# A conditioned attention and MLP block: ScalarE instead of GpSimd rounds the prepared weights to their high half

## The chip, the cores and the metric
The kernel runs on one core of a Trainium2 chip. The metric is the device time of one execution in microseconds. Five engines work beside each other, each through its own instructions in order: TensorE (PE; PEld is its weight loading), VectorE (DVE), ScalarE (ACT), GpSimd (POOL), and SyncE (SP), which here issues nearly all the DMAs.

## The reference
Input x has 64 batches of 128 tokens with 512 features, and a condition vector of 512 per batch. All is fp32.
```python
h = film(rmsnorm(x, norm1_w), cond, film1_w, film1_b)     # x * (1 + scale) + shift per batch
Q, K, V = h @ q_w + q_b, h @ k_w + k_b, h @ v_w + v_b
attn = softmax(einsum('bnd,bmd->bnm', Q, K) * D ** -0.5)
x = x_in + (einsum('bnm,bmd->bnd', attn, V) @ proj_w + proj_b)
h = film(rmsnorm(x, norm2_w), cond, film2_w, film2_b)
h = gelu(h @ mlp_w1 + mlp_b1, approximate=False) @ mlp_w2 + mlp_b2      # 512 -> 2048 -> 512
return x + h
```

## The kernel before, in words
Products are kept near fp32 accuracy by splitting an operand a into a high half hi (a rounded to the type fp32r) and a low half lo = a - hi, and adding three products, hi*hi, lo*hi and hi*lo. The MLP's two products are computed with seven block products instead of eight (a Strassen-Winograd scheme, P1 to P7), for which sums of the blocks of each weight matrix are needed. These sums and their halves don't depend on the tokens, so they are made once, in the attention stage, written to DRAM scratch (wu for w1, wd for w2), and streamed from there in the MLP.

A short set-up comes first. The attention stage then runs over 16 groups n = 0 to 15 of four batches (512 tokens), on all engines in a fixed written order:
- TensorE: g products (h times the joined query and key weights) 2 and 3, v product 0, scores, v products 1 to 3, transposes of the probabilities (L600), g product 0 of group n + 1, output products 0 and 1 (L609), g product 1 of n + 1, output products 2 and 3. The output products need the transposed probabilities in SBUF (pT_sb). Group 1 also computes the second FiLM product, between v product 2 and v product 3.
- ScalarE: copies g, modulates h of the next group (L761), keep_v(n,0), squares of x of group n + 2 (L753), four exponentials (L866), rounds h of the next group to its high half (L770), keep_v(n,1) to keep_v(n,3) (copies of the value products out of PSUM, L778), copies the transposed probabilities (pT_sb, L886), and the first two g of the next group.
- VectorE: adds output 2 and 3 of group n - 1 to x (L988), key terms (L979, L982), scales x of group n + 1 by the row of reciprocal norms (L957) and modulates it, maxima of the scores, scaling of the probabilities, low half of h (L971), adds output 0 and 1 of group n.
- GpSimd: norm1(n + 2), the reciprocal norms (L461, L464). In groups 1 to 8 it also prepares chunk c = n - 1 of the weights: sum_weights (four block sums, L481 to L486, once the chunk's source w_src has landed) and seven times split_weights, of which each casts the high half into the buffer w_out (L497) and then subtracts it for the low half (L499). norm1(n + 2) stands between the third and the fourth of the seven. PREP_ORDER gives their order: P1, P2 and P4 take a block of w_src itself, P5, P6, P7 and P3 one of the four sums w_sum. w_out has 8 buffers; the cast into one that was used waits for its store.
- SP, at the start of group n: x2 store, second half, of group n - 1 (L286, waits for the addition of output 3 of group n - 1); the seven weight stores of chunk n - 2 (L316; so a chunk is stored one group after it was made); two loads of the source of chunk n - 1 (L301 for w1, L305 for w2), into the single buffer w_src; load of xT of group n + 2; load of x_tok of group n + 3; store of the norms of group n + 2 (L291, waits for GpSimd) and, when that has landed, the load of their row (L295, broadcast); x2 store, first half, of group n.

In group 9 nothing is prepared; SP then loads the first pair of groups for the MLP (hn, L327) once all weight stores have landed, and ScalarE squares it in that group (L787), between keep_v(9,3) and the copy of the transposed probabilities. The MLP follows, 8 pairs of groups; GpSimd there adds residuals and forms norms.

The semaphores that the change touches: w_mixed counts the block sums (4 per chunk), w_hi the high halves, w_split the low ones (7 per chunk each), w_stored the stores of each w_out buffer, film_full the FiLM products.

Of the kernel before, what the change touches and what calls it, by code (L numbers as in the profile page):

```python
# [37 lines left out]
WOUT = 8  # L38
# [40 lines left out]
def cond_block_kernel(nc, x, xT, cols, condT, wqT, wkT, wvT, wp, f1w, f2w, w1, w2, outT, x2T, wu, wd, rs, rs2):  # L79
# [22 lines left out]
    with ExitStack() as ctx:  # L102
# [105 lines left out]
        def weight_blocks(c):  # L208

            if c < CHUNKS // 2:  # L210
                def view(k, r):
                    return w1_src[:, k:k + 2, r, :].rearrange("p t (j c) -> p j t c", c=P)
                return view(0, 0), view(2, 0), view(0, 1), view(2, 1)

            def view(r, d):
                return w2_src[:, :, r, d:d + 2 * P].rearrange("p j (t c) -> p j t c", c=P)
            return view(0, 0), view(1, 0), view(0, 2 * P), view(1, 2 * P)

        def x2_halves(n):

# [225 lines left out]
        @block.gpsimd  # L446
        def _(pool):
            nc.gpsimd.memset(ident[:], 0.0).then_inc(ident_zero, 1)
            pool.wait_ge(ident_zero, 1)
            nc.gpsimd.affine_select(out=ident[:], in_=ident[:], compare_op=ALU.not_equal, fill=1.0,  # L450
                                    base=0, pattern=[[-1, P]], channel_multiplier=1).then_inc(ident_done, 1)
            nc.gpsimd.memset(probs[:, 0, :], 1.0).then_inc(const_done, 1)
            nc.gpsimd.memset(minus_half[:], -0.5).then_inc(const_done, 1)
            nc.gpsimd.memset(eps_sum[:], EPS * D).then_inc(const_done, 1)
            pool.wait_ge(const_done, 3)
            nc.gpsimd.tensor_copy(ones_r[:], probs[:, 0, :]).then_inc(ones_r_done, 1)

            def norm1(m):
                pool.wait_ge(summed, GB * m + GB)
                wait_used(pool, rstd_stored, 16 * m)  # L460
                nc.gpsimd.tensor_tensor(rstd[:], sumsq[:], eps_sum[:].broadcast_to([P, GB]),  # L461
                                        ALU.add).then_inc(eps_added, 1)
                pool.wait_ge(eps_added, m + 1)
                nc.gpsimd.tensor_tensor(rstd[:], rstd[:], minus_half[:].broadcast_to([P, GB]),  # L464
                                        ALU.pow).then_inc(rstd_done, 1)

            def norm2(m):
                pool.wait_ge(stat_read, m + 1)
                wait_used(pool, rstd2_stored, 16 * m)
                nc.gpsimd.tensor_tensor(rstd2[:], sumsq2[:], eps_sum[:].broadcast_to([P, 2 * GB]),  # L470
                                        ALU.add).then_inc(eps2_done, 1)
                pool.wait_ge(eps2_done, m + 1)
                nc.gpsimd.tensor_tensor(rstd2[:], rstd2[:], minus_half[:].broadcast_to([P, 2 * GB]),
                                        ALU.pow).then_inc(rstd2_done, 1)

            def sum_weights(c):

                a11, a12, a21, a22 = weight_blocks(c)
                s1, s2, s3, s4 = (w_sum[q][:] for q in ("P5", "P6", "P7", "P3"))
                pool.wait_ge(w_src_loaded, 32 * c + 32)  # L480
                nc.gpsimd.tensor_tensor(s1, a21, a22, ALU.add).then_inc(w_mixed, 1)  # L481
                nc.gpsimd.tensor_tensor(s3, a11, a21, ALU.subtract).then_inc(w_mixed, 1)
                pool.wait_ge(w_mixed, 4 * c + 1)
                nc.gpsimd.tensor_tensor(s2, s1, a11, ALU.subtract).then_inc(w_mixed, 1)
                pool.wait_ge(w_mixed, 4 * c + 3)
                nc.gpsimd.tensor_tensor(s4, a12, s2, ALU.subtract).then_inc(w_mixed, 1)  # L486

            def split_weights(c, i):
                q, u = PREP_ORDER[i], 7 * c + i
                a11, a12, _, a22 = weight_blocks(c)  # L490
                src = {"P1": a11, "P2": a12, "P4": a22}[q] if q in ("P1", "P2", "P4") else w_sum[q][:]
                both = w_out[u % WOUT]
                if q == "P5":
                    pool.wait_ge(w_mixed, 4 * c + 4)
                if u >= WOUT:
                    pool.wait_ge(w_stored[u % WOUT], 16 * (u // WOUT))
                nc.gpsimd.tensor_copy(both[:, :, :, 0, :], src).then_inc(w_hi, 1)  # L497
                pool.wait_ge(w_hi, u + 1)
                nc.gpsimd.tensor_tensor(both[:, :, :, 1, :], src, both[:, :, :, 0, :].bitcast(F32),  # L499
                                        ALU.subtract).then_inc(w_split, 1)  # L500

            norm1(0)
            norm1(1)
            for n in range(GROUPS):
                if n == 11:
                    norm2(0)
                if 1 <= n <= CHUNKS:
                    if n == 1:
                        pool.wait_ge(film_full, 2)
                    sum_weights(n - 1)  # L510
                    for i in range(7):
                        if i == 3:
                            norm1(n + 2)
                        split_weights(n - 1, i)
                elif n + 2 <= LAST:
                    norm1(n + 2)

            def add_residual(p, into, rows, half, source, ready, count):

                pool.wait_ge(ready, count)  # L520
                for dt in range(2):
                    block_ap = into[:, 2 * rows + dt, TOK * half:TOK * half + TOK]
                    nc.gpsimd.tensor_tensor(block_ap, source[:, dt, :], block_ap, ALU.add).then_inc(pre_added, 1)  # L523

            for p in range(PAIRS):
                if p < PAIRS - 1:
                    norm2(p + 1)
                pool.wait_ge(b2_added, 8 * p + 8)
                add_residual(p, xres, 0, 1, u2, down_u2, 2 * p + 2)
                add_residual(p, xres, 1, 0, u2, down_u2, 2 * p + 2)  # L530
                add_residual(p, xres, 1, 1, vsum, down_v, 2 * p + 2)
# [216 lines left out]
        def _(act):  # L748
# [16 lines left out]
            def h_high(m, k):  # L765
# [3 lines left out]
                    act.wait_ge(h_done_act, 2 * m + k - 1)  # L769
                nc.scalar.copy(h_hi[m % 2][:, k, :], h[m % 2][:, k, :]).then_inc(h_hi_done, 1)  # L770

            def keep_g(n, j):
                act.wait_ge(g_full, GB * n + j + 1)
                nc.scalar.activation(g[:, j, :], gv[j][:], ACT.Identity, bias=wk_bq[:, j:j + 1]).then_inc(g_read, 1)  # L774

            def keep_v(n, b):
                act.wait_ge(v_full, GB * n + b + 1)
                nc.scalar.copy(v[:, b, :], gv[b][:]).then_inc(v_read, 1)  # L778
# [71 lines left out]

            for n in range(GROUPS):
                keep_g(n, 2)
                keep_g(n, 3)
                if n < LAST:
                    wait_used(act, scored, n)
                    if n == 0:
                        act.wait_ge(cols_read, 2)
                    modulate(n + 1, 2)
                    modulate(n + 1, 3)
                wait_used(act, out_full, GB * n)  # L860
                keep_v(n, 0)
                if n + 2 <= LAST:
                    sum_squares(n + 2)
                act.wait_ge(bias_done, n + 1)
                for b in range(GB):
                    nc.scalar.activation(probs[:, b, :], score_b[:, b, :], ACT.Exp, bias=exp_bias[:, b:b + 1],  # L866
                                         scale=SCALE, accum_out=den[:, b:b + 1]).then_inc(exp_done, 1)
                if n < LAST:
                    for k in range(KD):
                        h_high(n + 1, k)  # L870
                for b in range(1, GB):
                    keep_v(n, b)
                if n == 9:
                    squares_of_pair(0, sq_attn)
                if n == 13:
                    modulate_pair(0, 2)
                    modulate_pair(0, 3)
                if n == 14:
                    act.wait_ge(x2_stored[1], x2_halves(13))
                    for q in SPLIT_ORDER[:3]:  # L880
                        operand_high(0, q)
                if n == LAST:
                    for q in SPLIT_ORDER[3:]:
                        operand_high(0, q)
                act.wait_ge(pT_full, n + 1)
                nc.scalar.copy(pT_sb[:], pT[:]).then_inc(pT_read, 1)  # L886
                if n < LAST:
                    keep_g(n + 1, 0)
                    keep_g(n + 1, 1)
# [364 lines left out]
```

## Time and profile before

| | |
|---|---|
| time, median of 3 runs | 1972.0 us (1967.91 to 1976.14) |
| the profiled execution | 1968.15 us, span 1966.4 us |
| mean granted TensorE clock | 0.965 |
| busy: TensorE, VectorE, ScalarE, GpSimd | 94%, 64%, 44%, 15% |
| GpSimd instructions | 250, of them 56 casts (L497) and 56 subtractions (L499) of weights |
| attention stage | from about 70 us to about 610 us |
| weight preparation on GpSimd | 124 to 389 us |

How to read it: the span runs from the first to the last instruction of one execution; the time of the run has what lies around it as well. A row of a list of instructions begins with its start, then its duration, engine, line, operation, output and inputs, how many instructions are merged in it (x4), and in brackets the idle time of the engine just before and what ended it. Such a row's duration is that of the merged run.

### The profile page before, as it was taken

Reading aid. Unit: us, or ns where it says so; the run is one execution under the profiler, and the core shown is the slowest. Engines: PE = TensorE matmul, PEld = TensorE weight load, DVE = VectorE, ACT = ScalarE, POOL = GpSimd, SP = SyncE. Lnnn points to the kernel's source line nnn. Section 1 sums busy time; section 2 is a strip of 40 time slices with the busy share of each in tenths; the row PEclk is TensorE's granted clock in tenths of the full one; section 3 lists DMA queues with packets and bytes.
Section 4 is the critical chain, followed back from the end, with each engine's and each line's share of the span. In section 5 each row is a group of like instructions: output and inputs, shape, how many; then the busy total and the mean of one; then the engine's idle time right before and its main releaser. Section 6 shows DMA issues by size and latency. Waiting matters only on the chain.

```text
span 1966.4 us, 23402 instructions
## 1 busy us (share of the span) xinstructions
PE 1855.5 (94%) x8596; PEld 1534.7 (78%) x8596; DVE 1260.5 (64%) x1575; ACT 860.1 (44%) x1458; POOL 304.4 (15%) x250
## 2 busy tenths in 40 slices
PE   9999999989998999999899999989999998999998
PEld 8887887868787777777777777777877777787887
DVE  3455564645654687489468748946964894687467
ACT  3435343354633363355236335523633553363353
POOL 0044656600000002002000200200010020001002
PEclk7999999999999999999899999999998999999999
DMA  7237575653224667666666766676776667676775
GB/s 268 83 129 268 177 287 211 237 191 124 75 85 142 192 228 248 182 176 222 228 192 225 249 181 178 225 235 189 231 242 177 177 219 239 189 234 215 205 233 182
DMA packets 204992, 391.86 MB, mean 199 GB/s; under 512 B 22096, under 2 KB 26192, under 8 KB 204880
## 3 DMA queue, kind: packets, MB, share of 16 engines
q1 hardware_dynamic: 204592, 390.11, 61.6%
q8 instruction: 70, 1.15, 0.3%
q14 instruction: 42, 0.34, 0.1%
q10 hardware_dynamic: 288, 0.26, 0.0%
HBM read 327.32 MB, written 62.98 MB: 198 GB/s over the span
## 4 chain that ended last, share of the span: by engine, by line
PE 60%; DVE 14%; POOL 9%; DMA 8%; issue 4%; ACT 3%; SPq 2%; DVEq 0%; POOLq 0%; ACTq 0%
PE ps L639 25%; PE ps L659 13%; PE ps L537 8%; PE ps L667 7%; POOL w_out L499 4%; DMA ring<-wd_scratch 4%; DVE stage_lo L1130 3%; DVE hn L1006 3%; DMA w_src<-w_dram 3%; POOL w_out L497 2%; PE ps L609 2%; PE ps L573 1%; PE ps L578 1%; PE ps L574 1%; ACT hn L793 1%
## 5 line engine op out<-in xcount | busy, mean ns | idle before, releaser
L639 PE MATMUL ps<-op_hi_P,ring 128*128 128x512 f32 x1792 | 573.5, 402 | 15.4 <-ACT p_copy L898 12.9
L659 PE MATMUL ps<-stage_hi,ring 128*128 128x512 f32 x1792 | 447.6, 391 | 15.2 <-DMA ring<-wd_scratch 15.2
L639 PEld LDWEIGHTS ps<-op_hi_P,ring 128*128 128x128 f32 x1792 | 345.4, 195 | 97.2 <-ACT p_copy L898 17.8
L659 PEld LDWEIGHTS ps<-stage_hi,ring 128*128 128x128 f32 x1792 | 336.7, 189 | 90.3 <-DMA ring<-wd_scratch 18.6
L639 PE MATMUL ps<-op_lo_P,ring 128*128 128x512 f32 x896 | 357.4, 399 | 0.0
L819 ACT CAST stage_hi<-x 128x1024 fp32r<-128x1024 f32 x224 | 234.6, 1051 | 247.2 <-PE ps L659 229.2
L1130 DVE TENSOR_TENSOR stage_lo<-x,stage_hi 128x1024 fp32r<-128x1024 f32 x224 | 298.9, 1338 | 50.1 <-ACT stage_hi L819 50.0
L803 ACT ACTIVATE x<-x,vecs 128x512 f32<-128x512 f32 x192 | 138.1, 723 | 382.5 <-DVE x L1117 382.5
L667 PE MATMUL ps<-stage_lo,ring 128*128 128x512 f32 x896 | 245.2, 396 | 16.7 <-DVE stage_lo L1130 16.7
L667 PEld LDWEIGHTS ps<-stage_lo,ring 128*128 128x128 f32 x896 | 165.9, 189 | 62.7 <-DVE stage_lo L1130 29.4
L639 PEld LDWEIGHTS ps<-op_lo_P,ring 128*128 128x128 f32 x896 | 173.4, 194 | 37.7
L523 POOL TENSOR_TENSOR xres<-u,xres 128x512 f32<-128x512 f32 x32 | 70.7, 2239 | 824.5 <-DVE u L1141 824.5
L1117 DVE TENSOR_TENSOR x<-ps,u 128x512 f32<-128x512 f32 x128 | 86.4, 690 | 118.4 <-PE ps L639 118.0
L1136 DVE TENSOR_TENSOR x<-x,x 128x1024 f32<-128x1024 f32 x96 | 134.2, 1398 | 0.0
L1117 DVE TENSOR_TENSOR u<-ps,p_copy 128x512 f32<-128x512 f32 x64 | 44.2, 691 | 138.8 <-ACT p_copy L898 71.3
L774 ACT ACTIVATE g<-ps,wk_bq 128x512 f32<-128x512 f32 x64 | 44.1, 689 | 194.3 <-PE ps L578 194.3
L988 DVE SCALAR_TENSOR_TENSOR xT_in<-ps,attn_col,xT_in 128x512 f32<-128x512 f32 x64 | 47.8, 750 | 107.8 <-PE ps L609 103.6
L573 PE MATMUL ps<-h_hi,qk_hi 128*128 128x512 f32 x256 | 109.2, 427 | 2.4 <-ACT h_hi L770 2.4
L574 PE MATMUL ps<-h_hi,qk_lo 128*128 128x512 f32 x256 | 104.9, 410 | 0.0
L537 PE MATMUL ps<-vp_hi,h_hi 128*128 128x512 f32 x256 | 101.1, 395 | 0.0
L537 PE MATMUL ps<-vp_lo,h_hi 128*128 128x512 f32 x256 | 99.7, 389 | 0.0
L537 PE MATMUL ps<-vp_hi,h_lo 128*128 128x512 f32 x256 | 99.7, 389 | 0.0
(140 smaller groups left out, 2316.6 us busy)
## 6 DMA issues: line engine op xcount, KB each, us to landing
ring<-wu_scratch SPq DMA_DIRECT2D x448, 256.0 KB, 3.0
ring<-wd_scratch SPq DMA_DIRECT2D x448, 256.0 KB, 2.8
x_tok<-x_dram SPq DMA_DIRECT2D x16, 1024.0 KB, 9.0
xT_in<-xT_dram SPq DMA_DIRECT2D x16, 1024.0 KB, 8.8
x2T_scratch<-xT_in SPq DMA_DIRECT2D x32, 512.0 KB, 4.6
hn<-x2T_scratch SPq DMA_DIRECT2D x8, 2048.0 KB, 8.5
xres<-x2T_scratch SPq DMA_DIRECT2D x8, 2048.0 KB, 7.4
out_dram<-xres SPq DMA_DIRECT2D x32, 512.0 KB, 4.4
```

Source lines behind the costliest of these rows:

```text
L499: nc.gpsimd.tensor_tensor(both[:, :, :, 1, :], src, both[:, :, :, 0, :].bitcast(F32), ALU.subtract).then_inc(w_split, 1)
L537: mm = pe.matmul(bank_ap, a, b, start=t == 0, stop=t == len(steps) - 1)
L573: pe.matmul(gv[j][:], qk_hi[:, k, tokens(j)], h_hi[p][:, k, :], start=k == 0, stop=False)
L574: pe.matmul(gv[j][:], qk_lo[:, k, tokens(j)], h_hi[p][:, k, :], start=False, stop=False)
L639: mm = pe.matmul(to[:], wt, b, start=q in FRESH and t == 0, stop=t == len(steps) - 1, skip_group_check=True)
L659: mm = pe.matmul(bank(q, dt)[:], a[:, dt, part, :], stage_hi[r][:, e, :], start=q in FRESH and ss == 0 and e == 0 and part == 0, stop=Fals ...
L667: mm = pe.matmul(bank(q, dt)[:], a[:, dt, 0, :], stage_lo[r][:, e, :], start=False, stop=ss == 3 and e == 1, skip_group_check=True)
L803: nc.scalar.activation(into[:, jj, :], source, ACT.Gelu, bias=col("b1")[:, tile:tile + 1]).then_inc(sem_done, 1)
L819: nc.scalar.copy(stage_hi[st % 2][:], down_source[q][:, 2 * ss:2 * ss + 2, :]).then_inc(hi_done, 1)
L1117: dve.tensor_tensor(into, bank(q, s)[:], other[:, s, :], ALU.add).then_inc(sem_done, 1)
L1130: dve.tensor_tensor(stage_lo[st % 2][:], down_source[DOWN_ORDER[i]][:, 2 * ss:2 * ss + 2, :], stage_hi[st % 2][:].bitcast(F32), ALU.subtra ...
L1136: dve.tensor_tensor(into[:, at_s, :], a[:, at_s, :], b[:, at_s, :], ALU.subtract).then_inc(sem_done, 1)
```

## The change
ScalarE makes the high halves. The helper weight_source gives the block or sum that a split starts from. split_weights on GpSimd keeps only the subtraction, and waits for w_hi as before, which ScalarE now counts up. ScalarE makes high halves 0 to 2 after keep_v(n,1), 3 to 5 after keep_v(n,2), and 6 after the copy of the transposed probabilities. Its first in a chunk waits for all four sums (before, only the fourth cast did, in the engine's own order); the wait for the buffer's store moves with the casts. In group 1 it also waits for film_full, as GpSimd did and still does.

```diff
@@ (shared helpers)
+        def weight_source(c, i):
+            a11, a12, _, a22 = weight_blocks(c)
+            q = PREP_ORDER[i]
+            return {"P1": a11, "P2": a12, "P4": a22}[q] if q in ("P1", "P2", "P4") else w_sum[q][:]
@@ (GpSimd)
             def split_weights(c, i):
-                q, u = PREP_ORDER[i], 7 * c + i
-                a11, a12, _, a22 = weight_blocks(c)
-                src = {"P1": a11, "P2": a12, "P4": a22}[q] if q in ("P1", "P2", "P4") else w_sum[q][:]
-                both = w_out[u % WOUT]
-                if q == "P5":
-                    pool.wait_ge(w_mixed, 4 * c + 4)
-                if u >= WOUT:
-                    pool.wait_ge(w_stored[u % WOUT], 16 * (u // WOUT))
-                nc.gpsimd.tensor_copy(both[:, :, :, 0, :], src).then_inc(w_hi, 1)
+                u = 7 * c + i
+                src, both = weight_source(c, i), w_out[u % WOUT]
                 pool.wait_ge(w_hi, u + 1)
                 nc.gpsimd.tensor_tensor(both[:, :, :, 1, :], src, both[:, :, :, 0, :].bitcast(F32),
                                         ALU.subtract).then_inc(w_split, 1)
@@ (ScalarE)
+            def weight_high(c, i):
+                u = 7 * c + i
+                if i == 0:
+                    act.wait_ge(w_mixed, 4 * c + 4)
+                if u >= WOUT:
+                    act.wait_ge(w_stored[u % WOUT], 16 * (u // WOUT))
+                nc.scalar.copy(w_out[u % WOUT][:, :, :, 0, :], weight_source(c, i)).then_inc(w_hi, 1)
@@
                 for b in range(1, GB):
                     keep_v(n, b)
+                    if 1 <= n <= CHUNKS and b < 3:
+                        if n == 1:
+                            act.wait_ge(film_full, 2)
+                        for i in range(3 * b - 3, 3 * b):
+                            weight_high(n - 1, i)
@@
                 act.wait_ge(pT_full, n + 1)
                 nc.scalar.copy(pT_sb[:], pT[:]).then_inc(pT_read, 1)
+                if 1 <= n <= CHUNKS:
+                    weight_high(n - 1, 6)
```

## Rows read from the trace of the kernel before
**Rows 1.** The page: the chain that ended last, shares of the span by engine.
```profile
PE 60%; DVE 14%; POOL 9%; DMA 8%; issue 4%; ACT 3%; SPq 2%; DVEq 0%; POOLq 0%; ACTq 0%
```
**Rows 2.** All engines in order of time, group 9.
```profile
406.68 3.89 ACT L787 ACTIVATE sq_attn<-hn 128x1024 f32<-128x1024 f32 x4 [5.16 <-DMA hn<-x2T_scratch]
...
411.10 3.61 PE L609 MATMUL ps<-pT_sb,v 128*128 128x128 f32 x16 [7.93 <-ACT pT_sb L886]
...
418.41 1.65 DVE L988 SCALAR_TENSOR_TENSOR xT_in<-ps,attn_col,xT_in 128x512 f32<-128x512 f32 x2 [2.91 <-PE ps L609]
```
**Rows 3.** Busy time of each engine, clock and DMA in groups 1, 2, 9, 12.
```profile
99.80:137.29 37.49, 37.49 (x238) 33.58 (x237) 17.70 (x37) 14.59 (x37) 12.54 (x14) 1.00 0.30 99
137.29:168.40 31.11, 30.85 (x174) 26.40 (x173) 21.36 (x30) 14.26 (x37) 19.59 (x17) 1.00 0.75 262
...
377.92:420.06 42.14, 32.66 (x174) 27.88 (x173) 18.43 (x29) 18.04 (x41) 11.36 (x13) 0.92 0.67 237
...
482.53:512.85 30.32, 30.32 (x174) 26.46 (x173) 23.86 (x33) 14.60 (x37) 1.21 (x2) 1.00 0.38 113
```
**Rows 4.** TensorE in order of time, group 1: FiLM product and first output.
```profile
116.94 7.25 PE L537 MATMUL ps<-condT_sb,f2w_sb 128*128 128x64 f32 x64
...
130.04 1.95 PE L609 MATMUL ps<-pT_sb,v 128*128 128x128 f32 x16
```
**Rows 5.** Waits from 124 to 398 us: total, times, longest.
```profile
DVE h L957 <- DMA norm_row<-rs_scratch: 35.4, 8, 7.1
...
PE ps L600 <- DVE probs L1084: 12.4, 5, 3.2
```
**Rows 6.** GpSimd: one group of casts (busy, mean ns), then its timeline, groups 4-6.
```profile
L497 POOL CAST w_out<-w_sumP 128x512 fp32r<-128x512 f32 x32 | 24.2, 756 | 0.0
...
229.43 1.28 POOL L481 TENSOR_TENSOR w_sumP<-w_src 128x512 f32<-128x512 f32 x1 [14.04 <-DMA w_src<-w_dram]
...
234.50 0.60 POOL L497 CAST w_out<-w_src 128x512 fp32r<-128x512 f32 x1
235.18 1.28 POOL L499 TENSOR_TENSOR w_out<-w_src,w_out 128x512 fp32r<-128x512 f32 x1
...
262.75 1.63 POOL L481 TENSOR_TENSOR w_sumP<-w_src 128x512 f32<-128x512 f32 x1 [11.76 <-DMA w_src<-w_dram]
...
268.59 0.61 POOL L497 CAST w_out<-w_src 128x512 fp32r<-128x512 f32 x1
...
283.61 1.49 POOL L497 CAST w_out<-w_sumP 128x512 fp32r<-128x512 f32 x1
...
297.02 1.60 POOL L481 TENSOR_TENSOR w_sumP<-w_src 128x512 f32<-128x512 f32 x1 [9.82 <-DMA w_src<-w_dram]
```
**Rows 7.** SP's DMA issues in order of time, groups 5 and 6.
```profile
242.60 0.34 SPq L291 DMA_DIRECT2D rs_scratch<-rstd  x1
...
244.40 0.94 SPq L286 DMA_DIRECT2D x2T_scratch<-xT_in  x2
...
277.97 0.47 SPq L286 DMA_DIRECT2D x2T_scratch<-xT_in  x1
```
**Rows 8.** ScalarE, VectorE and TensorE in order of time, undisturbed groups 11, 12.
```profile
475.47 0.69 ACT L774 ACTIVATE g<-ps,wk_bq 128x512 f32<-128x512 f32 x1 [2.13 <-PE ps L578]
...
496.73 2.19 ACT L770 CAST h_hi<-h 128x512 fp32r<-128x512 f32 x4
...
480.89 1.64 DVE L988 SCALAR_TENSOR_TENSOR xT_in<-ps,attn_col,xT_in 128x512 f32<-128x512 f32 x2 [2.87 <-PE ps L609]
...
475.28 1.95 PE L609 MATMUL ps<-pT_sb,v 128*128 128x128 f32 x16
```
**Rows 9.** Windows around one burst; the last two columns are DMA share, GB/s.
```profile
244.40:262.75 18.35, 15.44 (x88) 13.01 (x87) 10.37 (x19) 9.75 (x30) 6.35 (x8) 0.95 0.93 345
...
248.00:250.00 2.00, 2.00 (x20) 2.00 (x20) 1.48 (x2) 0.00 (x0) 1.92 (x3) 1.00 1.06 410
```
**Rows 10.** The chain of waits in order of time: the last weight store.
```profile
391.13 7.50 DMA wd_scratch<-w_out
```

## The prediction, made before the changed kernel ran
> **What bounds the kernel now.** I read the page first. TensorE is busy for 94% of the span, but the chain that ended last goes through GpSimd for 9% and DMA for 8% of it [rows 1], and all GpSimd work of the changed helper lies in the attention stage. The stage is therefore read group by group. I cut it at the end of the last residual addition of each group (t0 of the next group: the second pair of L988 on VectorE, 418.41 + 1.65 = 420.06 for group 10 [rows 2]). The windows cut there [rows 3] give:
> - groups 2 to 8, with weight preparation: 137.29 to 377.92, 240.6 us, 34.4 each;
> - group 12, without preparation: 30.3, TensorE busy without a gap at clock 1.00. That is TensorE's own pace;
> - group 1: 37.5, which is 30.3 and the 7.25 of the second FiLM product [rows 3, 4]: already at TensorE's pace;
> - group 9: 42.1, although it prepares nothing.
>
> What holds groups 2 to 8 4.1 us above TensorE's pace is a ring that passes GpSimd, as the list of waits says [rows 5]: VectorE waits 35.4 us for the row of reciprocal norms, TensorE's transposes 12.4 us behind it. I follow one turn. The source of chunk 3 lands and GpSimd starts at 229.43; four sums take 5.1 us (first split 234.50), three splits of 1.92 us each (0.61 cast, 1.29 subtraction and the gaps) and the norm follow, and SP, which had waited, stores the norms at 242.60 [rows 6, 7]: 13.1 after the landing. SP then reloads the row, issues from 244.40 on two x2 stores, seven weight stores and the loads of the next source, which lands at 262.75 [rows 6, 7]. From the second x2 store (244.40 + 0.47) to that landing are 17.9 us; the next chunk has 277.97 to 297.02, 19.1 [rows 6, 7]. The other five chunks lie between, mean 18.4. The turn is 13.1 + 1.8 + 0.5 + 18.4 = 33.8, close to the 34.4 measured. So the casts on GpSimd are in this ring, but only the three ahead of the norm.
>
> **What the change removes.** GpSimd loses 7 casts per chunk: 32 of 0.756 us, 24.2 together, and 24 of 0.60 as at 234.50, 14.4: 38.6 us in all [rows 6]. Three of them, 1.8 us per turn, are in the ring above. If nothing else moved, the period would fall from 34.4 to 32.6: 7 x 1.8 = 12.6 us gained.
>
> **What it adds.** Seven copies per chunk on ScalarE. No row shows this very copy; ScalarE's rounding of a 128x512 tile in contiguous form takes 2.19 for four, 0.55 each [rows 8]. The new ones read and write pieces of 128 elements; the lower bound is 0.55, the upper the 0.69 that a 128x512 activation with a bias pointer takes [rows 8]. I take 0.55: nothing in the rows says that pieces of 128 cost anything. ScalarE has room for 3.9 us in a group (busy 14.3 of 31.1 in group 2 [rows 3]). So the work is cheap. The wait is not.
>
> **The added wait.** The first copy of a chunk waits for the four sums of the same chunk (w_mixed). It stands behind keep_v(n,1) and ahead of keep_v(n,2), keep_v(n,3), the copy of the transposed probabilities (L886) and keep_g. TensorE's output products (L609) need that L886 copy. I lay out one group from its t0.
>
> When ScalarE gets there: in an undisturbed group its rounding of h starts at 496.73 and keep_v(n,1) ends at 499.4, that is t0 + 16.9, with t0 = 480.89 + 1.64 = 482.53 [rows 8].
>
> When the sums are done: SP may not issue the next source load before the x2 store that needs t0 itself, and then the seven weight stores. Before, GpSimd's norm set this; now t0 does, because SP is free by then (see below). The x2 store can be issued at t0 + 0.1. In the old turn the core's DMA engines moved 345 GB/s from the x2 stores' issue at 244.40 to the landing at 262.75, 6.33 MB; at their full rate of 410 that is 15.4 us, so 2.9 of the 18.35 are the start's latency [rows 9]. The row's load, two x2 stores, seven stores and two loads make 0.26 + 1.05 + 3.67 + 1.05 = 6.03 MB, so some 0.30 MB of later loads mix in. The new burst ahead of the source's landing lacks the row and one x2 store: 0.52 + 3.67 + 1.05 + 0.30 = 5.54 MB, 13.5 us at 410 GB/s, so t0 + 0.1 + 2.9 + 13.5 = 16.5. The turn used for this is the shortest of seven, 0.5 under their mean: I take 17.0. Bounds: 15.5 with nothing mixed in (5.24 MB, 12.8) and little of the latency left over, and 19.1 if the load comes as late behind its x2 store as ever before. The sums take 5.1 to 5.8 (229.43 to 234.50, 262.75 to 268.59 [rows 6]); I take 5.3. Sums done: t0 + 22.3, 5.4 us after ScalarE arrived.
>
> Behind the wait: 0.1, then 3 copies (1.65), keep_v (0.5), 3 copies (1.65), keep_v (0.5), L886 (0.6) = 4.9: ends at t0 + 27.3. TensorE starts the output at t0 + 27.4. Undisturbed it starts at 475.28 with the next t0 at 482.53, 7.25 later; one period on that is t0 + 23.1 [rows 8]. So TensorE stands 4.3 us.
>
> From the output to the next t0: 7.25 undisturbed. Group 9 shows the same stall today: L886 sits behind squares that wait for a DMA, the output starts at 411.10 after 7.93 idle and takes 3.61 for its first 16 matmuls instead of 1.95; next t0 at 418.41 + 1.65 = 420.06, 8.96 later [rows 2, 8]. The granted clock of this group is 0.92, that of groups 1, 2 and 12, where TensorE has no such gap, 1.00 [rows 3]: part of group 9 ran at 1.2 GHz. For 4.3 us idle I take 8.8, bounds 7.25 and 8.96.
>
> New period: 22.3 + 0.1 + 4.9 + 0.1 + 8.8 = **36.2**, against 34.4.
>
> Does another link come later? GpSimd now splits behind ScalarE: subtractions of 1.29 [rows 6], three of them and the norm end near t0 + 28.4, the last near t0 + 34. SP stores the norms and is through with the row's load 1.8 us later, as before [rows 7], at t0 + 30.2. VectorE wants the row no earlier than the next t0, t0 + 36.2; that leaves 6.0 for the landing of half the bytes of a weight store, which takes 7.5 inside a full burst [rows 10], and here no burst is left: on time, so the 12.4 us at the transposes go, and I counted them as gone. All seven splits are ready before the next t0 + 0.1, SP too. w_out has 8 slots, and the stores of the chunk before are ahead of the source load in the same queue, so w_stored adds no wait.
>
> **Two places where the Trainium skill bears on it.** GpSimd's casts take 0.60 at the shortest and 1.49 at 283.61; the sums spread from 5.1 to 5.8 [rows 6]. The Trainium skill, GPSIMD Engine Reference, section 8, Key points, says GpSimd shares its SBUF interfaces with VectorE and contends with those of its instructions that have two SBUF inputs; by that rule the new sums, which fall after VectorE's work on h and the probabilities, would take 5.1, and the period would be 36.0 rather than 36.2.
> In group 9 TensorE stood 7.93 us for L886, which needs nothing of the squares ahead of it on ScalarE [rows 2]: ScalarE took nothing out of order. The Trainium skill, TensorE: Matmul & The Clock Gate, section Architectural detail, has ScalarE's queue as a strict FIFO; that is what speaks against the change, since with any overtaking the period would be 30.3.
>
> **The two ends of the stage.** Group 1: the source is there, the sums start when the FiLM product ends, at 124.2 [rows 4]; done at 129.3, L886 ends at 134.4, output at 134.5 instead of 130.04, then 8.8: next t0 at 143.3 instead of 137.29: +6.0. Groups 2 to 8: 7 x (36.2 - 34.4) = +12.6. Group 9: today the squares wait for the pair's load, and that for the last weight store, under way from 391.13 to 398.6 [rows 10]; they run 8.0 after that, at 406.68 [rows 2]. The stores lag the groups. In the changed kernel the stores start at t0 + 0.6: landed at t0 + 13.1 by bandwidth alone, 15.0 if the last one is issued at t0 + 7.5 and takes its 7.5 us of today; 14.2 taken, squares start 8.0 later at 22.2, 3.8 for them, L886 0.6, output at 26.6, next t0 at 35.4 instead of 42.1: -6.7. From group 10 on nothing differs, the MLP included: it holds none of this work.
> Sum: +6.0 + 12.6 - 6.7 = **+11.9 us** on the profiled execution: its 1968.15 (span 1966.4) becomes 1980.1. That execution lies 3.9 under the median of the runs; on the median of 1972.0 the forecast is 1984.
>
> **Rivals.**
> - A, faster: the source lands at bandwidth's pace and the stall is too short to lower the clock: 15.5 + 5.1 + 0.1 + 4.9 + 0.1 + 7.25 = 32.95 a period. 7 x -1.4 = -10, group 1 +4.5, group 9 -8: 14 less, 1958. The turning point is sums done at t0 + 20.5 (22.0 if the output runs at the full clock). For it: group 2 took 31.1 [rows 3], so SP's burst can be early. Against: no old turn shows less than 17.9. Chance 0.08.
> - B, no change: source at t0 + 16 with sums of 5.1 and an output phase of 8.3: 34.6 a period, group 1 +5.5, group 9 -7: about 1972. The gap left by VectorE's wait is only exchanged for one behind ScalarE. Chance 0.25.
> - C, much slower: source as late as 19.1, sums 5.8, copies 0.69 (5.8 in all with the keeps), 8.96: 39.9 a period, 7 x 5.5 = +38, group 1 +7, group 9 -5: 2012. Chance 0.11.
> - D, the change doesn't do what it says: the copies never wait and GpSimd's relief is all that remains, 30.3 a period: 7 x -4.1 - 9 = 38 less, 1934. Only if SP issues loads before t0, which its order forbids. Chance 0.03.
> - The forecast: 0.53, its own range 1976 to 1996.
>
> A measurement tells about 0.5%, 9.9 us, from no change. The forecast lies only 2 above that bound; about 0.07 of its 0.53 falls below. Slower 0.46 + 0.11 = 0.57; same 0.07 + 0.25 = 0.32; faster 0.08 + 0.03 = 0.11. The range takes in B and half of C: 1966 to 2006.
>
> **What the new profile would show.** GpSimd without casts in the stage, busy 38.6 us less. ScalarE waiting at the first copy of each chunk for L486's sum, some 5 us. TensorE idle before L609 behind L886, 4 us in each of groups 1 to 8; no idle at the transposes (L600). SP waiting at the x2 store for L988 and no longer at the norms. Cut at the same events, groups 2 to 8 of 36.2 each, group 9 of 35.4. The forecast is wrong if the source lands outside 15.5 to 19.1 after t0, if the copies take other than 0.55, if the output phase runs at the full clock, or if the idle at the transposes stays.

## The result, and the profile after

The changed kernel takes 1992.99 us (median of 4 runs, 1990.46 to 1995.13) against 1973.22 of the kernel before (4 runs): 1.0103 times as long, 95% interval 1.0077 to 1.0128, or 20 us slower. The forecast was 1984, 11.9 us slower than before, and its range 1966 to 2006. The profiled execution has a span of 1988.7 us against 1966.4, 22.3 more.

The page of the changed kernel, its span, busy times and the chain that ended last; GpSimd's share of the chain falls from 9% to 2% [rows 1], and ScalarE's and SP's rise:
```profile
span 1988.7 us, 23402 instructions
PE 1861.7 (94%) x8596; PEld 1543.0 (78%) x8596; DVE 1238.2 (62%) x1575; ACT 890.1 (45%) x1514; POOL 253.5 (13%) x194
PE 62%; DVE 14%; DMA 8%; ACT 5%; issue 4%; SPq 4%; POOL 2%; DVEq 0%; ACTq 0%
```
Cut at the same events as before, the attention stage divides so (us):

| groups | before | changed | difference | forecast |
|---|---|---|---|---|
| set-up, to t0 of group 1 | 99.80 | 97.56 | -2.2 | 0 |
| 1 | 37.5 | 43.2 | +5.7 | +6.0 |
| 2 to 8 | 240.6 (34.4 each) | 261.3 (37.3 each) | +20.6 | +12.6 |
| 9 | 42.1 | 37.8 | -4.3 | -6.7 |
| the rest of the span | 1546.3 | 1548.8 | +2.5 | 0 |

The windows of groups 4 and 9 of the changed kernel, to be read beside [rows 3]. Behind the length stand the busy times of PE, PEld, DVE, ACT and POOL, then the granted clock, the DMA share and GB/s. TensorE is idle 4.2 and 4.7 us and its granted clock is 0.91. GpSimd was busy 19.6 us in group 2 before and is busy 14.9 us here, ScalarE 14.3 and 18.0.
```profile
214.92:252.26 37.34, 33.10 (x174) 28.64 (x173) 15.86 (x29) 18.02 (x44) 14.90 (x13) 0.91 0.66 219
402.04:439.86 37.82, 33.17 (x174) 28.68 (x173) 15.86 (x30) 18.38 (x41) 1.20 (x2) 0.91 0.69 243
```
The waits from 124 to 440 us. The wait for the norms' row [rows 5] is gone, and so is TensorE's at the transposes. In their place stand ScalarE's first copy (line 777) behind GpSimd's last sum, and TensorE's output products (line 608) behind the copy of the transposed probabilities (line 898). Each row gives the total, how often, and the longest:
```profile
POOL w_sumP L487 <- DMA w_src<-w_dram: 146.9, 7, 21.9
...
ACT w_out L777 <- POOL w_sumP L492: 54.1, 8, 12.8
PE ps L608 <- ACT pT_sb L898: 38.6, 9, 4.8
```
Group 4 of the changed kernel in order of time (t0 = 214.92), first GpSimd, then ScalarE, TensorE, VectorE. The source lands at t0 + 17.6. The sums end at 237.67, t0 + 22.75. ScalarE had been there since 231.8, t0 + 16.9. Everything that ScalarE does from 237.70 on stood behind that wait, until line 898 ends at 242.37:
```profile
232.52 1.29 POOL L487 TENSOR_TENSOR w_sumP<-w_src 128x512 f32<-128x512 f32 x1 [21.37 <-DMA w_src<-w_dram]
...
236.38 1.29 POOL L492 TENSOR_TENSOR w_sumP<-w_src,w_sumP 128x512 f32<-128x512 f32 x1
...
231.22 0.60 ACT L785 COPY v<-ps 128x512 f32<-128x512 f32 x1
237.70 1.66 ACT L777 CAST w_out<-w_src 128x512 fp32r<-128x512 f32 x3 [5.88 <-POOL w_sumP L492]
239.27 0.58 ACT L785 COPY v<-ps 128x512 f32<-128x512 f32 x1
239.75 1.66 ACT L777 CAST w_out<-w_sumP 128x512 fp32r<-128x512 f32 x3
241.31 0.58 ACT L785 COPY v<-ps 128x512 f32<-128x512 f32 x1
241.78 0.59 ACT L898 COPY pT_sb<-ps 128x512 f32<-128x512 f32 x1
...
242.43 3.78 PE L608 MATMUL ps<-pT_sb,v 128*128 128x128 f32 x16 [4.24 <-ACT pT_sb L898]
...
250.62 1.64 DVE L1002 SCALAR_TENSOR_TENSOR xT_in<-ps,attn_col,xT_in 128x512 f32<-128x512 f32 x2 [3.62 <-PE ps L608]
```
SP in that group: the second x2 store is released by t0 (214.92), then the seven weight stores take 8.3 us to issue, then come the two loads of the source:
```profile
209.86 5.46 SPq L292 DMA_DIRECT2D x2T_scratch<-xT_in  x2
215.37 8.28 SPq L322 DMA_DIRECT2D wu_scratch<-w_out  x7
223.70 3.06 SPq L307 DMA_DIRECT2D w_src<-w_dram  x2
```
TensorE's granted clock around its gap, in windows of 1 us (the column before the last two). The array ends its last product near 238.2; the clock falls to the half level, 1.2 GHz, near 240.8 and comes back only near 247.6, 5.2 us after the output began:
```profile
240.00:241.00 1.00, 0.00 (x0) 0.00 (x0) 0.00 (x0) 1.00 (x3) 1.00 (x2) 0.89 0.00 0
241.00:242.00 1.00, 0.00 (x0) 0.00 (x0) 0.00 (x0) 1.00 (x3) 1.00 (x1) 0.50 0.00 0
...
246.00:247.00 1.00, 1.00 (x4) 0.81 (x4) 0.75 (x1) 0.00 (x0) 1.00 (x1) 0.50 0.67 33
247.00:248.00 1.00, 1.00 (x5) 0.80 (x4) 0.00 (x0) 0.00 (x0) 1.00 (x2) 0.70 0.71 156
```

### The profile page after: what moved, and what is told of

Read it like the earlier page. It is cut to its first block, busy times and chain, and to the rows that moved or that the text cites. A ratio compares the mean times of both kernels' runs of the same rounds, so it can differ in the third digit from the quotient of the medians.

```text
span 1988.7 us, 23402 instructions
## 1 busy us (share of the span) xinstructions
PE 1861.7 (94%) x8596; PEld 1543.0 (78%) x8596; DVE 1238.2 (62%) x1575; ACT 890.1 (45%) x1514; POOL 253.5 (13%) x194
## 4 chain that ended last, share of the span: by engine, by line
PE 62%; DVE 14%; DMA 8%; ACT 5%; issue 4%; SPq 4%; POOL 2%; DVEq 0%; ACTq 0%
PE ps L638 25%; PE ps L658 12%; PE ps L536 8%; PE ps L666 6%; DMA ring<-wd_scratch 5%; PE ps L608 4%; DVE stage_lo L1144 3%; SPq L322 3%; DVE hn L1020 3%; DMA w_src<-w_dram 3%; PE ps L572 2%; PE ps L573 2%; PE ps L577 2%; ACT w_out L777 1%; PE ps L552 1%
## 5 line engine op out<-in xcount | busy, mean ns | idle before, releaser
L658 PE MATMUL ps<-stage_hi,ring 128*128 128x512 f32 x1792 | 449.6, 392 | 17.3 <-DMA ring<-wd_scratch 17.3
L638 PEld LDWEIGHTS ps<-op_lo_P,ring 128*128 128x128 f32 x896 | 173.3, 193 | 37.8
L608 PE MATMUL ps<-pT_sb,v 128*128 128x128 f32 x512 | 79.7, 321 | 43.9 <-ACT pT_sb L898 43.9
L608 PEld LDWEIGHTS ps<-pT_sb,v 128*128 128x128 f32 x512 | 76.4, 232 | 50.6 <-ACT pT_sb L898 44.5
```

Of the source, the lines that this page charges most:

```text
L608: mm = pe.matmul(out_ps[d % 2][:, tokens(b)], v[:, b, tokens(d)], pT_sb[:, tokens(b)], start=True, stop=True)
L638: mm = pe.matmul(to[:], wt, b, start=q in FRESH and t == 0, stop=t == len(steps) - 1, skip_group_check=True)
L658: mm = pe.matmul(bank(q, dt)[:], a[:, dt, part, :], stage_hi[r][:, e, :], start=q in FRESH and ss == 0 and e == 0 and part == 0, stop=Fals ...
```

## Experiments

The kernel before was timed beside each of them: its median was 1968.57 us beside experiments 1 to 4, 1968.14 beside 5, 6 and the first pair of 7, and 1970.18 beside the repeat of that pair. A ratio is to these, and a difference from the changed kernel is the difference of the two ratios times 1970. Theory 1 is that of the forecast: the time goes into ScalarE's wait for sums whose source is loaded late, and into the slow clock behind TensorE's gap.

### 1. The source loads ahead of the weight stores (changed kernel)
```diff
+                    if 1 <= n <= CHUNKS:
+                        ...
+                        load_w_src(n - 1)
                     if 1 <= n - 1 <= CHUNKS:
                         store_w_chunk(n - 2)
-                    if 1 <= n <= CHUNKS:
-                        ...
-                        load_w_src(n - 1)
```


> The changed kernel, but SP issues the two loads of a chunk's source ahead of the seven weight stores of the chunk before. Nothing else differs; ScalarE's copies stay where the change put them. Theory 1 (the time goes into ScalarE's wait for sums whose source is loaded too late): the source lands near t0 + 7, the sums are done near t0 + 12.5, before ScalarE arrives at t0 + 16.9, so its wait and TensorE's 4.2 us idle before the output products go, groups 2 to 8 fall from 37.3 to about 30.5 us; group 1 (which waits for the FiLM product) and group 9 stay: 1993 - 48 = about 1945. Rival 2 (ScalarE's own added work ahead of the transposed probabilities costs the time, wait or not): period stays 36 or more, 1985 to 1993. Rival 3 (the casts' SBUF traffic slows the others): no change, 1993.

1942.96 us, ratio 0.9867 (0.9839 to 0.9896), where the changed kernel has 1.0103: 46 us less. Groups 2 to 8 take 30.3 each, group 1 43.4, group 9 36.0. In group 6 (t0 = 262.80) of this kernel the window, SP, GpSimd and ScalarE in order of time show how the wait went: the loads are issued at t0 + 0.5, the source is there at t0 + 7.5, and ScalarE's copies run without a gap behind keep_v(6,1), while TensorE is busy throughout at clock 1.00:
```profile
262.80:293.14 30.34, 30.34 (x174) 26.46 (x173) 20.05 (x30) 18.03 (x44) 15.23 (x13) 1.00 0.79 268
```
```profile
263.25 1.38 SPq L311 DMA_DIRECT2D w_src<-w_dram  x2
...
270.27 1.34 POOL L487 TENSOR_TENSOR w_sumP<-w_src 128x512 f32<-128x512 f32 x1 [9.14 <-DMA w_src<-w_dram]
...
280.20 0.60 ACT L785 COPY v<-ps 128x512 f32<-128x512 f32 x1
280.68 1.68 ACT L777 CAST w_out<-w_src 128x512 fp32r<-128x512 f32 x3
...
284.76 0.62 ACT L898 COPY pT_sb<-ps 128x512 f32<-128x512 f32 x1
```
ScalarE does the same 18.0 us of work here as in the changed kernel, at the same places. So neither that work nor its traffic costs TensorE anything; rivals 2 and 3 fall.

### 2. The same order on SP, with the casts still on GpSimd (kernel before)
The same edit, made in the kernel before.

> The kernel before, casts on GpSimd, with the same order on SP: source loads ahead of the weight stores. Theory 1: the load then waits for the last split (21.5 us after the landing), and lands about 6.5 after that; the ring is 28 us, under TensorE's 30.3, so groups 2 to 8 take about 30.5 to 31 instead of 34.4: about 1973 - 26 = 1947. If so, the placement of the casts was never what bounded the stage; the order on SP was. A rival in which GpSimd's own work bounds the stage expects 33 or more a group, 1965 or more.

1941.24 us, ratio 0.9869 (0.9848 to 0.989). Groups 2 to 8 take 31.0 on average (240.6 before became 216.7), group 1 37.5, group 9 37.6. The old ring was open as soon as the source no longer stood behind 3.7 MB of stores. GpSimd still casts here, and groups 5 to 8 take 30.3 each; only group 2 is long, 33.9, which experiment 7 comes back to. So the casts on GpSimd were not what held the stage at 34.4.

### 3. TensorE kept busy over the gap (changed kernel)
```diff
+                if 1 <= n <= CHUNKS + 1:
+                    pe.wait_ge(out_read, GB * n - 1)
+                    for t in range(18):
+                        pe.matmul(out_ps[0][:], qk_hi[:, t % KD, tokens(t % KD)], h_hi[(n + 1) % 2][:, t % KD, :],
+                                  start=True, stop=True)
                 output(n, 0)
```


> The changed kernel with 18 extra matmuls of 128x512 in groups 1 to 9, on TensorE just ahead of the output products, into the bank that the first of them overwrites; their result is used by nothing. They take about 4.1 us at 2.4 GHz, which is the idle time there. Theory 1 with its second term (after the idle time the output phase runs at 1.2 GHz for 3.4 us and more, 9.8 us instead of 7.25): the output starts when it did, at t0 + 27.5, but the clock stays at 2.4 GHz, so a group falls from 37.3 to about 34.8: 9 x 2.5 = 22 less, about 1971, and the granted clock of the stage near 1.00. A rival in which the output phase is long for another reason (SBUF traffic, the x2 store) expects no change or a slightly longer time, 1993 to 1998.

1968.52 us, ratio 1.0005 (0.9988 to 1.0022), where the changed kernel has 1.0103: 19 us less for 162 matmuls more. Groups 2 to 8 take 34.8. TensorE in group 4 (t0 = 208.67): the extra matmuls fill 4.24 us, the output starts at t0 + 27.3 as in the changed kernel, but its first 16 matmuls take 2.05 instead of 3.78, and the next t0 (243.35) comes 7.4 later instead of 9.8.
```profile
231.73 4.24 PE L722 MATMUL ps<-h_hi,qk_hi 128*128 128x512 f32 x18
235.97 2.05 PE L608 MATMUL ps<-pT_sb,v 128*128 128x128 f32 x16
```
```profile
208.67:243.35 34.68, 34.68 (x192) 29.75 (x191) 16.94 (x29) 18.04 (x44) 15.50 (x13) 1.00 0.70 236
```
So in groups 2 to 8 the clock is worth 2.5 us a group, and the wait itself remains.

### 4. All seven copies behind the copy of the transposed probabilities (changed kernel)
```diff
-                    if 1 <= n <= CHUNKS and b < 3:
-                        ...
-                        for i in range(3 * b - 3, 3 * b):
-                            weight_high(n - 1, i)
...
                 if 1 <= n <= CHUNKS:
-                    weight_high(n - 1, 6)
+                    if n == 1:
+                        act.wait_ge(film_full, 2)
+                    for i in range(7):
+                        weight_high(n - 1, i)
```


> The changed kernel with all seven copies of a chunk behind the copy of the transposed probabilities on ScalarE (only the seventh stood there). Same work, same waits, other place. Theory 1: nothing that TensorE needs soon stands behind the wait; output starts at t0 + 23.1, period 30.3 to 31.5 (the reciprocal norms come near t0 + 29 and their row near t0 + 34, about when VectorE wants it), group 1 back to 37.5: about 1993 - 45 - 6 = 1942. Rival 2 (added work on ScalarE) expects a gain of 3 us a group at most, 1970 or more, as the copies still stand ahead of keep_g. Rival 3: no change.

1956.6 us, ratio 0.9938 (0.9914 to 0.9962). The gap in front of the output went, as theory 1 said, and group 1 is back at 37.5. But 1956.6 is 15 above what I expected: groups 2 to 8 take 32.3 on average, from 30.3 to 36.9, and group 9 takes 45.5, where the changed kernel has 37.8. So some 8 of the 15 are group 9, where the squares wait 7.9 us for the pair's load, 2.8 in the changed kernel; why that load is later was not looked into. For groups 2 to 8 the waits from 124 to 420 us say why: VectorE waits for the norms' row again.
```profile
ACT w_out L777 <- POOL w_sumP L492: 40.3, 8, 7.3
...
DVE h L969 <- DMA norm_row<-rs_scratch: 26.1, 6, 6.0
...
PE ps L599 <- DVE probs L1096: 9.3, 5, 3.5
```
The norm ends 12.5 us after the source lands (224.59 to 237.10 in group 4) instead of 13.1, so with TensorE's wait gone the old ring bounds the stage again: 12.5 + 1.8 + 0.5 + 18.4 = 33.2, an estimate from the pieces of the kernel before. I had held the row to come just in time. It comes late: SP is held by the norms past t0 (in group 4 its x2 stores go out at 204.92, 7 us after t0), and the source lands at t0 + 26.9.

### 5. The copies without the wait (kernel before)
```diff
+            def spare_copy(u):
+                wait_used(act, spared, u - 1)
+                nc.scalar.copy(spare[u % 2][:], vp_hi[:, u % KD, :].bitcast(F32)).then_inc(spared, 1)
...
                     keep_v(n, b)
+                    if 1 <= n <= CHUNKS and b < 3:
+                        for i in range(3 * b - 3, 3 * b):
+                            spare_copy(7 * n - 7 + i)
```
and the seventh behind the copy of the transposed probabilities.

> The kernel before, plus seven rounding copies of 128x512 a group on ScalarE in groups 1 to 8, at the very places where the change put them, but from a weight that has long been there into spare memory: the change's added work on ScalarE without its wait; GpSimd keeps its casts, and nothing uses the copies. Theory 1: they put L886's copy 3.1 us later, of which 2.4 are hidden (in group 4 it ended at 228.9 and the output started at 231.3); 0.8 a group, about 1969 + 6 = 1975. Rival 2 (added work costs the time) expects the changed kernel's loss or more, 1988 to 1993.

1970.64 us, ratio 1.0007 (0.9991 to 1.0022): no difference. Groups 2 to 8 take 33.9, group 9 43.3. The traces say why: in groups 2 to 4 TensorE does stand 2.0 us ahead of the output products, behind ScalarE, but VectorE's wait for the norms' row, 35.4 us before [rows 5], is down to 7.9, and these groups take 34.4 to 34.5. The delay fell where the old ring left room.

### 6. The wait without the copies (kernel before)
```diff
                     keep_v(n, b)
+                    if 1 <= n <= CHUNKS and b == 1:
+                        act.wait_ge(w_mixed, 4 * n)
```


> The kernel before, with ScalarE's wait for the four sums (w_mixed) added behind its first copy of the value products in groups 1 to 8, and no copy: the change's wait without its work. Theory 1: the ring through GpSimd's norm is replaced by the one through t0: sums done at t0 + 22.7, then 0.1 + 1.6 to the end of L886's copy, 0.1, and 9.8 to the next t0: 34.3 us a group, which happens to be what the old ring takes (34.4); group 1 loses some 2, group 9 gains some 4 as in the changed kernel: about 1967. So the changed kernel's 37.3 needs both, wait and 3.1 us of copies behind it. A rival in which the wait alone explains the loss expects 1985 or more.

1973.41 us, ratio 1.0021 (1.0009 to 1.0034): 0.2% slower, where I expected no change. Groups 2 to 8 take 34.8 (34.3 expected), group 1 38.7, group 9 37.1. The waits of this kernel from 124 to 420 us: the ring is the new one, TensorE behind ScalarE's copy, and VectorE's wait for the norms' row is gone.
```profile
ACT v L778 <- POOL w_sumP L486: 51.9, 8, 12.8
...
PE ps L609 <- ACT pT_sb L888: 22.3, 9, 4.8
```
Copies alone cost nothing, the wait alone 4 us (by the ratio), both together 20. The stage takes the longer of two rings. The old one, through the norm, takes 34.4. The new one, through t0, SP's stores, the source and ScalarE, takes 34.8 without copies and 37.3 with the copies that stand in it. Term by term, on average of groups 2 to 8: the six copies put 3.1 us into the path; without GpSimd's casts the sums end 1.6 us sooner after t0 (22.75 against 24.3); and the output phase, from the output's start to the next t0, is 1.0 longer (9.8 against 8.9). That I had expected 34.3, near the 34.8, is partly luck: I had put the sums at 22.7 and the output phase at 9.8, and the two misses nearly cancel.

### 7. The repairs put together
From 1: the source loads first. From 4: group 1's copies behind the copy of the transposed probabilities, since there the sums wait for the FiLM product. And in group 9 the squares of the first pair moved behind that copy too.
```diff
-                if n == 9:
-                    squares_of_pair(0, sq_attn)
...
                 nc.scalar.copy(pT_sb[:], pT[:]).then_inc(pT_read, 1)
+                if n == 9:
+                    squares_of_pair(0, sq_attn)
```
With the casts on ScalarE:

> The changed kernel with source loads first on SP, group 1's copies behind L886's copy, and the squares of the first pair in group 9 behind it too. Theory 1: against the version with only the loads first (1943), group 1 falls from 43.4 to 37.5 and group 9 from 36.0 to 30.4: about 1943 - 11 = 1932.

1931.7 us, ratio 0.982 (0.9798 to 0.9843). Groups 2 to 9 take 30.3 each, group 1 37.5: TensorE's own pace everywhere.

With the casts on GpSimd (loads first, squares moved):

> The kernel before, casts on GpSimd, with source loads first on SP and the squares of the first pair in group 9 behind L886's copy. Theory 1: against the version with only the loads first (1941), group 9 falls from 37.6 to about 30.5: 1934, the same as the version with the casts on ScalarE within 0.3%: with the order of SP repaired the placement of the casts is worth nothing. A rival in which the relief of GpSimd is worth something once the waits are gone expects this one 4 or more us slower.

1937.05 us, ratio 0.9841 (0.9824 to 0.9859). I had expected 1934 and no difference from the casts on ScalarE; the rival had 4 us or more, and it held. Groups 4 to 9 take 30.3, but group 2 takes 35.5 and group 3 35.1. In group 2 VectorE's four low halves of h take 5.47 us, where they take 2.49 undisturbed; GpSimd is at its sums and its first casts and splits at that moment, and TensorE waits 2.9 us for them. In group 3 they take 5.5 us as well, beside GpSimd's later splits, and TensorE waits 2.2 us for them and 1.4 for the probabilities. First VectorE, then GpSimd:
```profile
156.53 5.47 DVE L971 TENSOR_TENSOR h_lo<-h,h_hi 128x512 fp32r<-128x512 f32 x4
```
```profile
156.14 1.62 POOL L486 TENSOR_TENSOR w_sumP<-w_src,w_sumP 128x512 f32<-128x512 f32 x1
157.69 1.08 POOL L497 CAST w_out<-w_src 128x512 fp32r<-128x512 f32 x1
```
The two intervals overlap, so both were run again with more rounds.

> The same kernel as e6_best_scalar, to settle on one chip, with more rounds, whether the placement of the casts is worth anything once SP's order is repaired. Its groups 2 to 8 all took 30.3 us. Theory 1: 1932, and 4 to 8 us under the version with the casts on GpSimd. A rival in which the 5 us between the two medians were scatter expects less than 2 us between them.

> The same kernel as e7_best_gpsimd. In its trace groups 2 and 3 took 35.5 and 35.1 us, since the casts on GpSimd keep SP from the second source load until 146 and push GpSimd's sums onto VectorE's low half of h (5.5 us instead of 2.5); the other groups took 30.3. Theory 1: again 35 in groups 2 and 3 and about 1937. The rival expects 1932 to 1934.

1927.5 us, ratio 0.9794 (0.9776 to 0.9812), and 1937.54 us, ratio 0.984 (0.9818 to 0.9862). The intervals no longer overlap: with the waits repaired, the casts on ScalarE are worth 5 us by the first pair of medians and 10 by the second; in both pairs of traces groups 2 to 8 are 10 us shorter (212.3 against 222.3 and 222.5). In the second trace with GpSimd's casts the long groups were 2 (34.0) and 4 (36.6), not 2 and 3; that some early groups are late is shown, and which they are varies. The best version is the one with the casts on ScalarE, 2% faster than the kernel before and 3% faster than the change as it was made.

## Why the prediction was right, point by point

The direction and every wait of the forecast came. The size was off: 22.3 us between the profiled executions, not 11.9. Of the 10.4 us by which the forecast was exceeded 8.0 are in groups 2 to 8 and 2.4 in group 9, and most of it is one term, the output phase.

- **What bounded the kernel**: a ring through the source, GpSimd's sums, three splits and the norm, and SP. Experiment 2 opens it without touching GpSimd's work. I followed the casts in it (1.8 us a turn) and did not say that the 18.4 us of the source's way, behind the seven stores, were the part worth the most. One reading in it was off: the longest of the seven turns from the second x2 store to the sums is 19.2 (210.21 to 229.43), not 19.1, and the mean 18.5; nothing hangs on it.
- **What the change removes**: GpSimd is busy 50.9 us less (304.4 to 253.5), of which 38.6 are the casts. The rest is in its subtractions (80.3 to 71.2 in all) and its reciprocal norms (23.5 to 19.4); that these were slower for running beside VectorE is likely, but was not tested. The sums take 5.15 in three of seven groups, 5.3 in one and 5.75 to 6.0 in three.
- **The copies on ScalarE**: 0.55 each, taken right (three in 1.66). Pieces of 128 elements cost nothing: the rounding of h, in contiguous form, takes as long.
- **The wait**: ScalarE arrives at t0 + 16.9 as forecast. The source lands at t0 + 17.3 on average of seven (17.0 forecast), the sums end at t0 + 22.75 (22.3), the output starts at t0 + 27.5 (27.4). This mechanism holds, and experiments 1, 4, 5 and 6 show it from four sides. One sign that I had named did not come: SP does wait for VectorE ahead of the x2 stores, 42.7 us in all, but it still waits for the norms, 134.1 us (143.2 before). It does so ahead of t0, so the ring does not pass there.
- **The output phase is the term that was too small**: 9.8 us from the output's start to the next t0 (8.98 in group 2, 9.67 to 10.17 in the others), not 8.8. I set 8.96 as its upper bound from the one stall of group 9 [rows 2], where the clock had fallen 3.5 us before the output and returned 3.3 after its start. In group 4 of the changed kernel it falls only 1.7 us before the output and stays down for 5.2 us of it. Experiment 3 shows that this is the clock. 7 x 1.0 is nearly all of the 8 us by which groups 2 to 8 exceed the forecast. One stall could not give a bound, since the idle time alone does not set the price. In group 13, which the change leaves alone, TensorE stands 4.1 us ahead of the output in every kernel, and its output phase takes from 8.98 us (before, 3.4 us of it at 1.2 GHz) to 10.14 (the repeat with GpSimd's casts, 5.9 us of it). In group 9 of experiment 5 it stands 8.5 us and takes 9.93. What decides between them is open. The first output products of these three, TensorE in order of time:
```profile
540.18 3.35 PE L609 MATMUL ps<-pT_sb,v 128*128 128x128 f32 x16 [4.10 <-ACT pT_sb L886]
```
```profile
507.60 3.78 PE L609 MATMUL ps<-pT_sb,v 128*128 128x128 f32 x16 [4.10 <-ACT pT_sb L884]
```
```profile
408.87 3.78 PE L611 MATMUL ps<-pT_sb,v 128*128 128x128 f32 x16 [8.49 <-ACT pT_sb L895]
```
- **Group 1**: +5.7 against +6.0.
- **Group 9**: -4.3 against -6.7. SP issued the pair's load at t0 + 13.7 (14.2 forecast), but it took 9.7 us to the squares instead of 8.0, and the output phase was again 9.9 instead of 8.8. The load of xT ahead of it on SP landed 3.9 us after the pair's load was issued, 2.7 in the kernel before; what the rest is, is open.
- **The rest** moved by -2.2 and +2.5 us, outside the groups; no step of mine has it, and it cancels. Over the twelve traces the set-up takes 97.0 to 100.8 us and the part behind group 9 1546.2 to 1553.6, so differences of this size say nothing of the change.
- **The rivals**: A and B needed a source at t0 + 16 or sooner; the earliest of seven was 16.5. C's source at 19.1 didn't come either, though its output phase, 8.96, was exceeded. The chance of 0.57 for slower was low for a mechanism in which only the output phase was off; its price had been put only 2 us above what a measurement can tell.

The rule of strict order on ScalarE, taken from the Trainium skill, TensorE: Matmul & The Clock Gate, section Architectural detail, agrees with the trace: keep_v(4,2) had its data before 237.7 and ran at 239.27, behind the waiting copies. Where GpSimd works beside VectorE's operations on two SBUF tensors both stretch (experiment 7), 2.49 to 5.47 us for VectorE's four and 0.61 to 1.08 for GpSimd's cast; with that the rule of the Trainium skill, GPSIMD Engine Reference, section 8, Key points, agrees as well. I had worked out from it that the sums would take 5.1, as VectorE would be through with the low halves of h. That was so in four of seven groups; in the other three the source landed 0.6 to 1.6 us sooner, the sums began beside the low halves and took 5.75 to 6.0.

## What to carry to other kernels

Before work is moved to an engine with room, look at what its first instruction waits for and what stands behind it in that engine's order: the copies alone (3 us in the path) cost nothing and the wait alone (5.6 us a group on average) 4 us in all, but together, in the path of TensorE's next operand, they cost 20 us. Where a stage is slower than its busiest engine, follow one turn of the ring and look for its longest piece; here it was a load queued behind stores that nobody was in a hurry for, and the order of two calls on SP was worth 26 us against the kernel before, with either placement of the casts.

## What the runs showed of the hardware that I had not expected

A gap of TensorE of 4.2 us cost 2.5 us more in the work behind it, through the granted clock at 1.2 GHz for 5.2 us of that work; one of 7.9 us cost 1.7, with 3.3 us at 1.2 GHz. That is no rule that a shorter gap costs more: gaps of 4.1 us in front of the same work cost 1.7 in one kernel and 2.9 in another, and one of 8.5 us cost 2.7. Short gaps cost as well: in groups 2 to 4 of experiment 5 TensorE's only gap of 2.0 us was followed by an output phase of 8.98 us instead of 7.25, and the clock fell 0.8 to 1.5 us after that work had begun. Filling the gaps with matmuls whose result nobody used made the changed kernel 19 us faster.

GpSimd and VectorE slow each other: four VectorE subtractions of 128x512 with both inputs in SBUF took 5.47 us beside GpSimd's sums and casts, 2.49 without, and a GpSimd cast 1.08 to 1.49 us instead of 0.61.
